# Layer norm of the next batch in two halves on ScalarE, its statistics in front of the output addition, the router's exponential one step later, rounding in front of gelu, and the output stored in quarters

## The chip, the core and the metric

One core of a Trainium2 chip runs the whole program. The time is the device time of one execution in microseconds (us); lower is better. The engines are TensorE (PE in the rows; its weight loads are PEld), VectorE (DVE), ScalarE (ACT), GpSimd (POOL) and SyncE (SP, which here only issues DMAs). Each works through its own list of instructions in order, and waits on semaphores.

## The reference

Everything is float32. There are 4 batches of 512 tokens with 256 features. In the attention part a query sees the 65 keys `i-64 <= j <= i`; the context gives keys and values.

```python
x = x + tanh(g_xattn) * attention(layernorm(x), ctx, wq, wk, wv, wo)   # 16 heads of 64, rotary, window 64
h = layernorm(x)
shared = einsum('tse,she->th', gelu(h @ shared_up), shared_down)       # 2 shared experts, 128 wide
probs  = softmax(h @ router_w.T)                                       # 16 routed experts
gate   = probs where among the 4 largest, else 0
routed = einsum('tre,rhe->th', gelu(h @ routed_up) * gate, routed_down)
x = x + tanh(g_ffn) * (shared + routed)
```

The kernel computes every one of the 18 experts for every token and multiplies a routed one by its gate, which is 0 for most tokens.

## The kernel before

**Products.** Every float32 operand of a projection is split into a rounded part (`xTh`, `wh`, `oTh`, made by ScalarE) and the rest (`xTl`, `wl`, `oTl`, a subtraction on VectorE or GpSimd), and each product is three matmuls (`product`, line 827).

**Attention.** Work is cut into 16 units `u` (batch `b = u // 4`, group of 4 heads `g`), and each unit into 4 steps, so that there are 64 steps `c` (one head each), with `k = c % 4` and a few steps to drain. A list `steps` says which jobs go with each step, and every engine walks through the same list. For head `c`: PE makes the scores (`psS`, L990; two heads at a time, at even `c`), VectorE takes the row maxima (L781), ScalarE the exponentials (L563), VectorE inverts their sum (L791), GpSimd divides (L422), PE transposes (`psT`, L1002), ScalarE copies them (`pT`, L572), PE multiplies by the values (`psO`, L1021), ScalarE rounds the result (`oTh`, L578) and VectorE makes its rest (`oTl`, L795). Jobs `q`, `k`, `v` are the next unit's projections, job `y` the output projection of the unit before, whose result VectorE adds to `x` (L749). PE writes the jobs into two pairs of banks, `ring`.

**Layer norm of batch `b+1`** is made while batch `b` is in attention: job `stat` (VectorE: L630, L633, from `x`; then four small GpSimd instructions, L446 to L455, which make `rstd` and `shift`), job `norm` (ScalarE, four ACTIVATEs `xn<-x,shift,rstd`, L553), job `xT` (PE transposes `xn`, ScalarE rounds, VectorE makes the rest). The layer norm of the expert part has the same jobs with `n = B + b`; the first of them, `n = B = 4`, falls into the attention of the last batch (steps 53, 55 and 59).

**The last unit** (steps 60 to 63) also holds the router of batch 0: `r` (PE L967; four VectorE instructions up to `lex`, L670, semaphore `r_sub`; then the exponential `lexp` on ScalarE, L544), `pick_a` and `pick_b` (VectorE, the four largest), `gT` (PE transposes the gate).

**Experts.** 72 experts `n` (18 in each batch) follow each other. On PE expert `n` is `up(n)` (6 matmuls 128x512, `ring[0]`) and then `down(n - 2)` (12 matmuls 128x256 into the sums). In between come ScalarE's `gelu(n)` (L495, `act_g`, shown as `sneg`), VectorE's multiplication by the gate (`gated`, L706, `prob<-sneg,arena`, routed experts only), ScalarE's rounding (`round_gated`, L511, `oTh`) and VectorE's rest (`rest_gated`, L714, `oTl`, semaphore `f_lo`, for which `down` waits). `round_gated(n)` also waits for `down(n - 2)`, which read the same buffer. Table `after` puts the jobs of the next batch's layer norm and router behind certain experts. At a batch's end VectorE adds the sums to `x` in two halves (job `z`, L770) and SyncE stores each half.

ScalarE has to load a function table (`ACT_TABLE_LOAD`) when it goes from exponential to gelu and back. The copies and the rounding need none.

## Time and profile before

| | |
|---|---|
| runs, median (lowest to highest) | 548.89 us (548.44 to 549.3), 3 runs |
| the profiled execution: its own time | 548.71 us |
| the profiled execution: span from the first to the last instruction | 546.9 us |
| PE busy | 517.7 us, 95% |
| PEld, DVE, ACT, POOL busy | 84%, 60%, 56%, 52% |
| chain that ended last | PE 77%, POOL 9%, DVE 5%, issue 4%, ACT 3% |
| mean granted TensorE clock | 0.984 |

The profiled execution's own time is 1.8 us above its span, and 0.2 us under the median. A share of the whole span says little here: what matters is in which stretches PE stands still, and for whom. A matmul's end is modelled, and matmuls overlap, so that the wait that a row shows in brackets is a little less than what was lost.

### The profile page before, as it was taken

To read this page: it belongs to the slowest core of one execution; us is meant where nothing else is said; L and a number is where in the kernel's file an instruction comes from. 1 tells how busy PE (TensorE), PEld (TensorE's weight loads), DVE (VectorE), ACT (ScalarE), POOL (GpSimd) and SP (SyncE) were. 2 spreads that over 40 slices of the span, in tenths; PEclk is the share of its full clock that TensorE was granted. 3 is DMA by queue.
4 is the path that set the end of the run, shared out by engine and by line. 5 is a ranking of instruction groups with operands and counts; after the bars stand their busy time and mean duration, and the time that the engine had idled before them with its cause. 6 is when DMAs were issued, how large, how long until landed. Compare 5 with 4: busy or idle time off the path is not lost.

```text
span 546.9 us, 13117 instructions
## 1 busy us (share of the span) xinstructions
PE 517.7 (95%) x4906; PEld 457.7 (84%) x4906; DVE 327.7 (60%) x1047; ACT 306.5 (56%) x860; POOL 284.7 (52%) x231
## 2 busy tenths in 40 slices
PE   7667989999999999999999889999999999999997
PEld 5556878998899888988889778989998999899996
DVE  5866756566756676657565736564555455544444
ACT  3264666566675657766666575764454445444332
POOL 4668999797889778988797635440100010000000
PEclk9997999999999999999999799999999999999999
DMA  7422224110131011102111237305400450054001
GB/s 251 163 74 59 58 62 145 35 37 1 35 112 36 2 37 35 37 15 61 35 37 31 61 101 266 96 27 180 170 1 0 151 199 2 1 178 172 0 1 38
DMA packets 20173, 41.02 MB, mean 75 GB/s; under 512 B 2896, under 2 KB 3152, under 8 KB 20112
## 3 DMA queue, kind: packets, MB, share of 16 engines
q1 hardware_dynamic: 20112, 40.20, 23.4%
q8 instruction: 39, 0.64, 0.5%
q14 instruction: 22, 0.18, 0.1%
HBM read 30.62 MB, written 2.23 MB: 60 GB/s over the span
## 4 chain that ended last, share of the span: by engine, by line
PE 77%; POOL 9%; DVE 5%; issue 4%; ACT 3%; DMA 1%; POOLq 0%; ACTq 0%; DVEq 0%
PE ring L827 52%; PE psS L827 9%; PE psO L1021 6%; PE psS L990 5%; PE psT L1002 4%; POOL arena L416 2%; POOL prob L422 2%; POOL arena L418 2%; POOL arena L406 1%; POOL wl L430 1%; DVE arena L656 1%; PE psT L967 1%; POOL arena L409 1%; DVE oTl L714 1%; ACT pT L572 1%
## 5 line engine op out<-in xcount | busy, mean ns | idle before, releaser
L827 PE MATMUL ring<-xTh,wh 128*128 128x512 f32 x272 | 111.3, 409 | 3.3 <-DVE wl L727 1.7
L827 PE MATMUL ring<-xTh,wl 128*128 128x512 f32 x272 | 107.3, 394 | 0.0
L827 PE MATMUL ring<-xTl,wh 128*128 128x512 f32 x272 | 106.9, 393 | 0.0
L495 ACT ACTIVATE sneg<-ring 128x512 f32<-128x512 f32 x72 | 43.2, 600 | 102.1 <-PE ring L827 99.4
L706 DVE TENSOR_TENSOR prob<-sneg,arena 128x512 f32<-128x512 f32 x64 | 44.8, 699 | 75.1 <-ACT sneg L495 73.4
L827 PE MATMUL ring<-wh,oTh 128*128 128x256 f32 x272 | 78.3, 288 | 1.7 <-DVE oTl L714 0.9
L827 PE MATMUL ring<-wl,oTh 128*128 128x256 f32 x272 | 76.8, 282 | 0.0
L827 PE MATMUL ring<-wh,oTl 128*128 128x256 f32 x272 | 76.6, 282 | 0.0
L422 POOL TENSOR_TENSOR prob<-prob,rinv 128x512 f32<-128x512 f32 x64 | 66.7, 1042 | 14.9 <-DVE rinv L791 14.8
L827 PEld LDWEIGHTS ring<-xTh,wh 128*128 128x128 f32 x272 | 51.3, 189 | 13.3 <-issue 3.2
L827 PEld LDWEIGHTS ring<-xTh,wl 128*128 128x128 f32 x272 | 51.2, 188 | 12.0
L827 PEld LDWEIGHTS ring<-xTl,wh 128*128 128x128 f32 x272 | 51.4, 189 | 7.2
L563 ACT ACTIVATE prob<-sneg,nmax 128x128 f32<-128x128 f32 x128 | 49.6, 391 | 12.6 <-DVE nmax L781 12.6
L827 PEld LDWEIGHTS ring<-wh,oTh 128*128 128x128 f32 x272 | 51.2, 188 | 4.6 <-DVE oTl L714 1.5
L572 ACT ACTIVATE pT<-psT 128x512 f32<-128x512 f32 x64 | 37.9, 592 | 30.0 <-PE psT L1002 30.0
L430 POOL TENSOR_TENSOR wl<-raw,wh 128x512 fp32r<-128x512 f32 x27 | 37.4, 1391 | 32.6 <-ACT wh L524 32.6
L563 ACT ACTIVATE prob<-arena,nmax 128x128 f32<-128x128 f32 x128 | 49.7, 395 | 5.2 <-DVE nmax L781 3.5
L827 PEld LDWEIGHTS ring<-wl,oTh 128*128 128x128 f32 x272 | 51.3, 189 | 1.5
L827 PEld LDWEIGHTS ring<-wh,oTl 128*128 128x128 f32 x272 | 51.3, 189 | 0.0
L714 DVE TENSOR_TENSOR oTl<-prob,oTh 128x512 fp32r<-128x512 f32 x64 | 45.0, 703 | 6.3 <-ACT oTh L511 6.3
L578 ACT ACTIVATE oTh<-psO 128x512 fp32r<-128x512 f32 x32 | 19.2, 600 | 52.0 <-PE psO L1021 52.0
L749 DVE SCALAR_TENSOR_TENSOR x<-ring,tg,x 128x1024 f32<-128x1024 f32 x16 | 20.5, 1284 | 46.1 <-PE ring L827 46.1
(117 smaller groups left out, 1268.6 us busy)
## 6 DMA issues: line engine op xcount, KB each, us to landing
arena<-gate_scratch SPq DMA_DIRECT2D x64, 256.0 KB, 6.6
raw<-in_e SPq DMA_DIRECT2D x18, 256.0 KB, 2.6
raw<-in_w SPq DMA_DIRECT2D x16, 256.0 KB, 3.0
arena<-arena SPq DMA_DIRECT2D x16, 256.0 KB, 3.1
arena<-arena SPq DMA_DIRECT2D x16, 192.0 KB, 3.5
craw<-in_ctx SPq DMA_DIRECT2D x4, 512.0 KB, 4.2
x<-in_x SPq DMA_DIRECT2D x4, 512.0 KB, 4.0
out<-x SPq DMA_DIRECT2D x8, 256.0 KB, 2.7
```

The lines of the kernel that those rows point to most:

```text
L422: pool.tensor_tensor(prob[:, c % BUFS, :, :], prob[:, c % BUFS, :, :], rinv[:, c % BUFS, :].unsqueeze(2).to_broadcast([P, TT, P]), ALU.mul ...
L430: pool.tensor_tensor(wl[:, slot(n), :], raw[:, n % RAW, :], wh[:, slot(n), :].bitcast(F32), ALU.subtract).then_inc(w_lo_p, 1)
L495: act.activation(act_g[:, n % 2, :], ring[0][:, n % 2, :], ACT.Gelu).then_inc(f_gelu, 1)
L563: last = act.activation(prob[:, c % BUFS, t, :], sneg[c % BUFS][:, t, :], ACT.Exp, bias=nmax[:, c % 4, t:t + 1], scale=-1.0, accum_out=rsu ...
L572: act.activation(pT[:, c % 4, :, :], psT[:, :, :], ACT.Copy).then_inc(p_out, 1)
L706: dve.tensor_tensor(act_f[:, n % 2, :], act_g[:, n % 2, :], gate_bc[:, r, :], ALU.mult).then_inc(f_mul, 1)
L714: dve.tensor_tensor(lo, src[:, n % 2, :], hi.bitcast(F32), ALU.subtract).then_inc(f_lo, 1)
L749: dve.scalar_tensor_tensor(x[:, b, :, :].rearrange("p t d -> p (t d)"), both_banks(job)[:, :, :].rearrange("p a n -> p (a n)"), tg[:, 0:1] ...
L827: last = pe.matmul(out, a, b, start=start and i == 0 and j == 0, stop=stop and i == n - 1 and j == 2, skip_group_check=check)
L990: last = pe.matmul(psS[odd][e * W:(e + 1) * W, t, :], qT[rows, u % 2, h // 2, blk * W:(blk + 1) * W], kT[rows, u % 2, h // 2, blk * W:(blk ...
L1002: last = pe.transpose(psT[:, t, :], prob[:, c % BUFS, t, :], ident[:, :])
L1021: last = pe.matmul(psO[h * DH:(h + 1) * DH, blk * W:(blk + 1) * W], v[:, u % 2, t, head * DH:(head + 1) * DH], pT[:, (2 * p + h) % 4, t, e ...
```

## The change

- Attention: job `stat` of the next batch now stands in front of job `y` in step `k = 3, g = 1`; `norm` is cut into `norm_a` (step `k = 0, g = 2`) and `norm_b` (step `k = 1, g = 2`), two ACTIVATEs each. For the first layer norm of the expert part `stat` moves from step 53 to 51 (in front of `y`), `norm` from step 55 to halves at 52 and 53.
- The router's exponential becomes a job of its own, `rexp`: for batch 0 it goes from the end of step 60 to step 61, behind the copy of the transposed probabilities; for the other batches from behind expert 9 to behind expert 10. The layer norm's jobs among the experts each go one expert later.
- `expert(n)`: ScalarE rounds expert `n-1` before it takes gelu of `n`, and VectorE makes the rest of `n-1` before it multiplies `n` by its gate.
- PE issues the `up` of the last expert together with that of the one before.
- `z` and the stores go in four quarters (128x256) instead of two halves.

```diff
+            if (k, g) == (3, 1) and b + 1 < B:
+                jobs.append(("stat", b + 1))
+            if c == CHUNKS - 13:
+                jobs.append(("stat", B))
             if k == 3 and u >= 1:
                 jobs.append(("y", u - 1))
...
-            if k == 3 and g == 1 and b + 1 < B:
-                jobs.append(("stat", b + 1))
             if k == 0 and g == 2 and b + 1 < B:
-                jobs.append(("norm", b + 1))
-            jobs += {(UNITS - 3, 1): [("stat", B)], (UNITS - 3, 3): [("norm", B)],
+                jobs.append(("norm_a", b + 1))
+            if k == 1 and g == 2 and b + 1 < B:
+                jobs.append(("norm_b", b + 1))
+            jobs += {(UNITS - 3, 0): [("norm_a", B)], (UNITS - 3, 1): [("norm_b", B)],
...
-            for e, kind in ((2, "stat"), (4, "norm_a"), (5, "norm_b"), (7, "xT"), (9, "r"), (11, "pick_a"),
-                            (12, "pick_b"), (14, "gT")):
+            for e, kind in ((3, "stat"), (5, "norm_a"), (6, "norm_b"), (8, "xT"), (9, "r"), (10, "rexp"),
+                            (11, "pick_a"), (12, "pick_b"), (14, "gT")):
...
             def expert(n):
+                if 1 <= n <= N:
+                    round_gated(n - 1)
                 if n < N:
                     gelu(n)
-                if 1 <= n <= N:
-                    round_gated(n - 1)
...
+                if c == CHUNKS - 3:
+                    do(("rexp", 0))
...
             def expert(n):
+                if 1 <= n <= N:
+                    rest_gated(n - 1)
                 if n < N and experts[n][1] >= NS:
                     gated(n)
-                if 1 <= n <= N:
-                    rest_gated(n - 1)
...
-                    for half in range(2):
-                        dve.wait_ge(down_pe, 2 * NE * (n + 1) - 1 + half)
+                    for t in range(TT):
+                        dve.wait_ge(down_pe, 2 * NE * (n + 1) - 1 + t // 2)
...
             def expert(n):
-                if n < N:
+                if n < N - 1:
                     up(n)
+                if n == N - 2:
+                    up(n + 1)
                 if n >= 2:
                     down(n - 2)
```

ScalarE around the first layer norm of the expert part, steps 55 and 56 before, 52 and 53 now (`xn` is the layer norm, `pT` the copy for which PE's values wait). Before:

```order
L553 ACTIVATE xn<-x,shift,rstd 128x256 [waits xT_pe,ln_rstd]
L553 ACTIVATE xn<-x,shift,rstd 128x256 x3
L572 ACTIVATE pT<-psT 128x512 [waits oT_pe,p_pe]
L578 ACTIVATE oTh<-psO 128x512 [waits y_pe,oT_pe]
L563 ACTIVATE prob,rsum<-sneg,nmax 128x128 [waits p_pe,s_max]
```

Now:

```order
L556 ACTIVATE xn<-x,shift,rstd 128x256 [waits xT_pe,ln_rstd]
L556 ACTIVATE xn<-x,shift,rstd 128x256
L575 ACTIVATE pT<-psT 128x512 [waits oT_pe,p_pe]
L566 ACTIVATE prob,rsum<-sneg,nmax 128x128 [waits p_pe,s_max]
L566 ACTIVATE prob,rsum<-sneg,nmax 128x128 x3
L556 ACTIVATE xn<-x,shift,rstd 128x256 [waits xT_pe,ln_rstd]
L556 ACTIVATE xn<-x,shift,rstd 128x256
L575 ACTIVATE pT<-psT 128x512 [waits oT_pe,p_pe]
```

Four ACTIVATEs stood in front of one copy; now two stand in front of each of two copies, one step apart.

ScalarE among the experts of a middle batch, around the router's exponential (`sneg` is gelu's output, `oTh` the rounding). Before:

```order
L495 ACTIVATE sneg<-ring 128x512 [waits f_lo,up_pe]
L511 ACTIVATE oTh<-prob 128x512 [waits down_pe,f_mul]
L544 ACT_TABLE_LOAD
L544 ACTIVATE lexp<-lex 128x64 [waits r_sub]
L495 ACT_TABLE_LOAD [waits f_lo]
L495 ACTIVATE sneg<-ring 128x512 [waits up_pe]
L511 ACTIVATE oTh<-prob 128x512 [waits down_pe,f_mul]
```

Now:

```order
L514 ACTIVATE oTh<-prob 128x512 [waits down_pe,f_mul]
L498 ACTIVATE sneg<-ring 128x512 [waits f_lo,up_pe]
L547 ACT_TABLE_LOAD
L547 ACTIVATE lexp<-lex 128x64 [waits r_sub]
L514 ACTIVATE oTh<-prob 128x512 [waits down_pe,f_mul]
L498 ACT_TABLE_LOAD [waits f_lo]
L498 ACTIVATE sneg<-ring 128x512 [waits up_pe]
L514 ACTIVATE oTh<-prob 128x512 [waits down_pe,f_mul]
```

The rounding of an expert now stands in front of the next expert's gelu, one of them between the two table loads, and the exponential stands one expert later.

PE near the end of the program: the end of `up(70)` (`xTh,wh` and its like, 128x512) and what follows it. Before:

```order
L827 MATMUL ring<-xTh,wh 128x512
L827 MATMUL ring<-xTl,wh 128x512
L827 MATMUL ring<-xTh,wl 128x512
L827 MATMUL ring<-wh,oTh 128x256 [waits f_lo]
L827 MATMUL ring<-wl,oTh 128x256
```

Now:

```order
L832 MATMUL ring<-xTh,wh 128x512
L832 MATMUL ring<-xTl,wh 128x512
L832 MATMUL ring<-xTh,wl 128x512
L832 MATMUL ring<-xTh,wh 128x512 [waits f_gelu]
L832 MATMUL ring<-xTl,wh 128x512
```

`down(68)` stood behind `up(70)`; now `up(71)` stands there, and all four of the last `down`s stand behind it.

## Rows read from the trace of the kernel before

**Rows 1.** Windows: length, busy of PE, PEld, DVE, ACT, POOL; granted clock; DMA share, GB/s
```profile
52.50:92.50 40.00, 36.78 (x440) 32.04 (x439) 26.15 (x101) 28.50 (x93) 39.24 (x32) 1.00 0.30 85
92.50:272.50 180.00, 180.00 (x2185) 159.99 (x2184) 118.11 (x470) 116.72 (x410) 150.61 (x113) 1.00 0.15 39
```

**Rows 2.** Timeline of PE, early attention: start, length, instruction, [idle before, releaser]
```profile
91.53 0.47 PE L827 MATMUL ring<-xTh,wh 128*128 128x512 f32 x1 [0.29 <-POOL xTl L435]
```

**Rows 3.** Timeline of PE, steps 55 and 56: its waits there
```profile
279.55 0.36 PE L827 MATMUL ring<-wh,oTh 128*128 128x256 f32 x1 [0.62 <-DVE oTl L795]
282.79 0.65 PE L1002 MATMUL psT<-ident,prob 128*128 128x128 f32 x4 [0.16 <-POOL prob L422]
285.01 1.15 PE L1021 MATMUL psO<-pT,arena 128*64 128x64 f32 x32 [0.54 <-ACT pT L572]
```

**Rows 4.** Timeline of DVE and of ACT, steps 51 to 55
```profile
264.17 1.28 DVE L749 SCALAR_TENSOR_TENSOR x<-ring,tg,x 128x1024 f32<-128x1024 f32 x1 [3.73 <-PE ring L827]
275.26 1.40 DVE L630 BATCH_NORM_STATS2 stats<-x 128x6 f32<-128x256 f32 x4
...
273.36 0.60 ACT L572 ACTIVATE pT<-psT 128x512 f32<-128x512 f32 x1 [1.09 <-PE psT L1002]
282.41 2.07 ACT L553 ACTIVATE xn<-x,shift,rstd 128x256 f32<-128x256 f32 x4
```

**Rows 5.** Timeline of PE, steps 60 to 63
```profile
309.22 1.09 PE L1002 MATMUL psT<-ident,prob 128*128 128x128 f32 x4 [1.45 <-ACT pT L572]
310.24 1.99 PE L990 MATMUL psS<-arena 64*64 64x128 f32 x32
315.64 0.36 PE L827 MATMUL ring<-wh,oTh 128*128 128x256 f32 x1
```

**Rows 6.** Timeline of ACT, steps 60 and 61
```profile
308.34 0.26 ACT L544 ACTIVATE lexp<-lex 128x64 f32<-128x64 f32 x1 [0.77 <-DVE lex L670]
308.50 0.58 ACT L572 ACTIVATE pT<-psT 128x512 f32<-128x512 f32 x1
...
311.04 0.58 ACT L572 ACTIVATE pT<-psT 128x512 f32<-128x512 f32 x1
```

**Rows 7.** Windows, columns as in rows 1: the stretch of the lower clock
```profile
308.25:314.75 6.50, 5.53 (x72) 4.55 (x73) 4.29 (x36) 3.85 (x14) 2.83 (x3) 0.50 0.15 45
```

**Rows 8.** Chain that ended last: start, length, what
```profile
494.68 43.86 PE ring L827 x276
```

**Rows 9.** Timeline of PE, end of `up(11)` and start of `down(9)` in batch 2
```profile
468.96 0.40 PE L827 MATMUL ring<-xTl,wh 128*128 128x512 f32 x1
469.19 0.40 PE L827 MATMUL ring<-xTh,wl 128*128 128x512 f32 x1
469.90 0.39 PE L827 MATMUL psS<-wh,oTh 128*128 128x256 f32 x1 [0.32 <-DVE oTl L714]
```

**Rows 10.** Timeline of ACT, behind expert 9 of batch 1
```profile
411.79 0.26 ACT L544 ACTIVATE lexp<-lex 128x64 f32<-128x64 f32 x1 [1.72 <-DVE lex L670]
412.06 1.28 ACT L495 ACT_TABLE_LOAD   x1
413.36 0.60 ACT L495 ACTIVATE sneg<-ring 128x512 f32<-128x512 f32 x1
```

**Rows 11.** Timeline of ACT, DVE and PE, the last two experts and the end
```profile
538.56 0.60 ACT L495 ACTIVATE sneg<-ring 128x512 f32<-128x512 f32 x1 [1.73 <-PE ring L827]
540.05 0.63 ACT L511 ACTIVATE oTh<-prob 128x512 fp32r<-128x512 f32 x1 [0.38 <-PE ring L827]
...
539.19 0.69 DVE L706 TENSOR_TENSOR prob<-sneg,arena 128x512 f32<-128x512 f32 x1 [1.55 <-ACT sneg L495]
540.72 0.69 DVE L714 TENSOR_TENSOR oTl<-prob,oTh 128x512 fp32r<-128x512 f32 x1 [0.23 <-ACT oTh L511]
542.98 1.46 DVE L770 SCALAR_TENSOR_TENSOR x<-ring,tg,x 128x512 f32<-128x512 f32 x2 [1.57 <-PE ring L827]
...
540.54 0.39 PE L827 MATMUL ring<-wh,oTh 128*128 128x256 f32 x1 [0.58 <-DVE oTl L714]
```

More of the change, by code:

```diff
@@ L360, in store @@
             def store(b):
-                for half in range(2):
-                    sp.wait_ge(z_out, 2 * b + half + 1)
-                    sp.dma_start(out_d[b][:, 2 * half:2 * half + 2, :],
-                                 x[:, b, 2 * half:2 * half + 2, :]).then_inc(out_done, 16)
+                for t in range(TT):
+                    sp.wait_ge(z_out, TT * b + t + 1)
+                    sp.dma_start(out_d[b][:, t, :], x[:, b, t, :]).then_inc(out_done, 16)
             def do(job):
@@ L382, in _ @@
                 do(job)
-            sp.wait_ge(out_done, 16 * 2 * B)
+            sp.wait_ge(out_done, 16 * TT * B)
         @block.gpsimd
@@ L541, in do @@
                     expert(n)
-                elif kind == "r":
+                elif kind == "rexp":
                     act.wait_ge(r_sub, n + 1)
@@ L766, in do @@
                 elif kind == "z":
-                    for half in range(2):
-                        dve.wait_ge(down_pe, 2 * NE * (n + 1) - 1 + half)
-                        tokens = x[:, n, 2 * half:2 * half + 2, :].rearrange("p t d -> p (t d)")
-                        dve.scalar_tensor_tensor(tokens, sums(n, half), tg[:, 1:2], tokens,
+                    for t in range(TT):
+                        dve.wait_ge(down_pe, 2 * NE * (n + 1) - 1 + t // 2)
+                        dve.scalar_tensor_tensor(x[:, n, t, :], sums(n, t // 2)[:, t % 2 * D:t % 2 * D + D],
+                                                 tg[:, 1:2], x[:, n, t, :],
                                                  ALU.mult, ALU.add).then_inc(z_out, 1)
@@ L884, in down @@
                     if b >= 2:
-                        pe.wait_ge(z_out, 2 * (b - 1))
+                        pe.wait_ge(z_out, TT * (b - 1))
                     elif b:
```

## The prediction

> **What bounds the kernel now.** I read the windows first. From 92.5 to 272.5 us PE is busy for all of 180.00 us at full clock [rows 1]: nothing that another engine does there shows in the time unless PE comes to wait. Among the experts the chain of waits has one piece of 276 matmuls in 43.86 us [rows 8]; an expert has 18, so one takes 2.86 us and PE is again the bound. What can be won is the time in which PE waits, so I took PE's timeline and kept the rows with a bracket. In a row of matmuls one starts .23 us after the other although each lasts .40 (468.96, 469.19); the one behind the wait should start at 469.42 and starts at 469.90, so a bracket of .32 has cost .48 [rows 9]. I add this refill (.05 to .16) to each bracket. PE waits in five places: before 91.5 us, at 279 to 285, at 304 to 325, four times among the experts, and before the last two `down`s.
>
> **The early layer norm (steps 7 to 9): 0.** PE has 3.2 us without work from 52.5 to 92.5, some of it behind ScalarE's four `xn`, which are now two and two. But GpSimd is busy for 39.24 of these 40 us [rows 1], and what PE waits for at the end, at 91.53, is GpSimd's `xTl` [rows 2]. The change gives GpSimd the same instructions in nearly the same order. PE comes there earlier and waits longer. If GpSimd were not the wall, the gain would be up to 3; I take 0, since the 0.8 us that GpSimd does not work are scattered, and allow 0.4. Batches 2 and 3 have their layer norms in the stretch without a wait: 0, too.
>
> **The layer norm for the experts (now steps 51 to 53): -1.55.** Three waits: .62 for `oTl` behind the statistics on VectorE, .16 for a division, .54 for `pT` behind the four `xn` (282.41 to 284.48) [rows 3, 4]. With refill (.07, .16, .06) that is 1.6. In the new places: VectorE stands idle 3.73 us before the output addition at 264.17, and the statistics (1.40 and the aggregation, under 2 in all) fit into that; the addition is not late [rows 4]. GpSimd's `rstd` and `shift` come two steps earlier and are out of the way of the division. On ScalarE two `xn` take half of 2.07, 1.04 us. The first two run in the idle time before a `pT`. The second two stand before the `pT` at 273.36, which has 1.09 us of idle time in front of it [rows 4]: all but used up by 1.04, so I leave a new wait of .05, up to .4 if `shift` comes late. 1.6 - .05 = 1.55.
>
> **The router's exponential in the last unit: -0.7 or -1.75.** PE stood idle 1.45 us, from 307.77 to 309.22 [rows 5], because `pT` of head 58 was queued behind the exponential, which waited for `lex` until 308.34 and let `pT` start at 308.50 [rows 6]. Now `pT` goes first and starts at about 307.8: .7 us earlier. The second `pT` (311.04) stands behind a softmax and a weight rounding and moves by some .35 only, to an end at 311.25. What follows hangs on the clock. In this stretch, 308.25 to 314.75, the granted clock is .50, the 1.2 GHz level [rows 7]; it fell after PE had run the router's 16 matmuls of 32 columns and then stood idle. At this clock the transposes and the scores (1.99 us) hide the wait for the second `pT`, and the gain is .7. If the clock stays up, transposes and scores are over at about 310.05, PE waits until 311.25 for `pT`, values take 1.1, then `oTh` and `oTl` .60 and .69 with hand-over, and the output projection, before at 315.64 [rows 5], starts at 313.9: the gain is 1.75. PE still runs the 16 narrow matmuls and still stands .7 us behind them, so I take the fall as the likelier: .7. Later waits there (the first gelu's table load) move along unchanged.
>
> The Trainium skill, TensorE: Matmul & The Clock Gate, Part 1, says that the gate follows how busy TensorE has been, not the program; by this rule either outcome is open, and it would make the sum 1.05 larger if the clock held. The rows at .50 agree with a gate that answers to idleness.
>
> **The experts: -1.8.** Four waits for `f_lo`, at `down(3)` of batch 0 and `down(9)` of batches 0, 1 and 2, of .45 to .48 with refill, 1.9 together; the last of them stands in [rows 9]. An `up` takes six times .23, so a `down` about 1.45. Counted from the end of `up(n)`, `down(n)` starts at 5.7. Before, the rounding stood behind gelu(n+1) and the rest behind the next gate, which ends at 2.86 + 1.5: rest done at 5.05, a cushion of .65. Now: gelu until .8 (.60 long), gate until 1.5 (.69), rounding until 2.25 (.63; it may start when `down(n-2)` is over, at about 1.6), rest until 3.0; gelu of `n+1` starts at 3.05, so the rounding in front does not delay it. The cushion grows to 2.7. What is queued behind the rounding is gelu, behind that `up` two experts later; neither is late while the loop gelu, gate, rounding (.60 + .69 + .63 and hand-overs, 2.1) stays below 2.86. The exponential no longer waits for `lex` (1.72 us before [rows 10]), but its two table loads now stand behind gelu(10) and behind round(10): counted from the end of `up(10)`, load 0.7 to 2.0, exponential to 2.3, rounding to 2.9, load to 4.2, gelu(11) to 4.8, gate to 5.5, `pick_a` (1.2 us) to 6.7, rest(11) to 7.4; `down(11)` starts at 8.5. In batch 0, with weight roundings between and a slower `pick_a`, rest(11) ends at about 8.5: no cushion, for which I take .1, at most .4. The transposes `xT` come one expert nearer to the router; their rests end about .2 before PE needs them, so again 0 to .2 for each batch.
>
> In the trace gelu starts .02 us after the table load of 1.28 [rows 10]. The Trainium skill, ScalarE: Activation LUTs, What ACT_TABLE_LOAD costs, gives 1283 ns for the load, and agrees, but 1380 ns of drain with it, which no row here shows. By the page every switch would hold ScalarE 1.4 us longer; that is the last rival's story.
>
> **The end: -0.05.** Before, `down(70)` waited .58 (.74 with refill) and `down(71)` started 1.45 later, at 541.98 [rows 11]. Now both `up`s are over at 538.36 less one `down` (1.45), at 536.9, and `down(68)` ends at 538.35. Round(70) needs `down(68)`: 538.5 to 539.15; rest(70) to 539.85; `down(70)` starts at 539.9, .65 earlier. But gelu(71), which could start at 537.1, is queued behind round(70): to 539.65; its gate stands behind rest(70): to 540.5; rounding to 541.15, rest to 541.85; `down(71)` starts at 541.9. The wait has moved from one `down` to the other and .05 is won. This is a price of rounding first together with the early `up`.
>
> **Stores in quarters: 0.** Two halves of `z` take 1.46 us [rows 11]. A width of 1024 takes 1.28 [rows 4], of 512 .73, so 256 about .46, and two of them .2 more than one half. The last store then starts .2 later with half the bytes; from the end of `z` (544.44) to the end of the span (546.9) a half's store took 2.4. Bounds: .2 of a loss if bytes cost nothing, .4 of a gain if they cost as in a rate fitted to these. I take 0.
>
> **Sum.** 1.55 + .7 + 1.8 + .05 = 4.1 off the profiled execution's 548.7: 544.6. Against the median, .2 higher, 544.8; I say **544.6**.
>
> **Rivals.**
> - *Forecast: all waits named go, the clock falls again.* 543.9 to 545.3. Chance .50.
> - *The clock holds in the last unit.* For it: .75 us less idling behind the router's matmuls. Against: the narrow matmuls stay, and a new wait of 1.2 us follows. 544.6 - 1.05 = 543.5. Chance .24.
> - *The waits come back in part.* Norm_b late by .4, batch 0 without cushion (.4), `xT` late three times (.6), and PE's longer wait before 91.5 brings the low clock there, which would make some of PE's work after it late by about 1. 544.6 + 2.2 = 546.8. For it: each cushion is .2 or less. Chance .14.
> - *The change does nothing*: the waits at 279 and among the experts turn up elsewhere in full, e.g. because VectorE, not ScalarE's order, sets `f_lo`. 548.7. Chance .04.
> - *Slower: the table switch costs more in its new place*, between two roundings. If each load held ScalarE 1.28 longer, gelu(11) and rest(11) would be 2.56 later: waits of 2.5, 1.5 and 1.5 in the three batches, 544.6 + 5.5 = 550.1. It makes the kernel slower than before once the extra passes about 1.0 us for a load. Against it: .02 [rows 10]. Chance .08.
>
> **Numbers.** What a measurement of this kernel can tell from no change is about 0.2% (1.1 us). Faster: .50 + .24 + .14 = .88; same .04; slower .08. The range 543.0 to 546.9 holds the first three.
>
> **What the changed profile would show.** No bracket for `oTl` or `pT` on PE at the place of `norm` (now about 270 to 275); a bracket before the transposes behind the router of .7 instead of 1.45, and in the windows the clock level there; no `f_lo` bracket among the experts except perhaps at `down(11)` of batch 0; PE still released by GpSimd's `xTl` near 91.5; a bracket of up to .6 at `down(71)` and about .1 at `down(70)`. The forecast is wrong if PE waits before `r`, if GpSimd's stretch gets shorter, or if brackets appear behind the table loads.

## The result, and the profile after

| | before | after |
|---|---|---|
| runs of one chip, median (lowest to highest) | 548.95 us (548.44 to 549.33), 7 runs | 545.16 us (544.74 to 547.05), 7 runs |
| ratio, 95% interval | | 0.9942 [0.9925, 0.9958] |
| profiled execution: own time, span | 548.71, 546.9 | 545.07, 543.2 |
| PE, DVE, ACT, POOL busy | 95%, 60%, 56%, 52% | 95%, 62%, 58%, 52% |
| mean granted clock | 0.984 | 0.991 |

The changed kernel is faster by 0.58%. The runs of after lie on two levels, four at 544.7 to 545.2 (clock .991 or .987) and three at 546.7 to 547.1 (.981); the profiled one is of the lower.

The windows of after, columns as in [rows 1]; the last one is the stretch behind the router, which answers to [rows 7]:

```profile
52.50:92.50 40.00, 36.87 (x440) 32.03 (x439) 26.84 (x102) 29.26 (x96) 38.78 (x31) 1.00 0.30 84
92.50:272.50 180.00, 180.00 (x2185) 160.00 (x2184) 119.46 (x477) 117.05 (x408) 152.28 (x118) 1.00 0.15 39
307.25:313.25 6.00, 3.79 (x76) 3.02 (x77) 5.69 (x36) 4.75 (x21) 2.84 (x3) 1.00 0.14 46
```

PE's timeline of after, six of its waits from 92 us on (start, length, instruction, [idle before, releaser]):

```profile
92.04 0.47 PE L832 MATMUL ring<-xTh,wh 128*128 128x512 f32 x1 [1.10 <-POOL xTl L438]
...
307.25 0.63 PE L1009 MATMUL psT<-ident,prob 128*128 128x128 f32 x4 [0.78 <-ACT pT L575]
...
309.88 1.15 PE L1028 MATMUL psO<-pT,arena 128*64 128x64 f32 x32 [0.97 <-ACT pT L575]
...
313.27 0.36 PE L832 MATMUL ring<-wh,oTh 128*128 128x256 f32 x1 [1.27 <-DVE oTl L800]
...
366.45 0.39 PE L832 MATMUL psS<-wh,oTh 128*128 128x256 f32 x1 [0.23 <-DVE oTl L719]
...
538.09 0.38 PE L832 MATMUL ring<-wh,oTh 128*128 128x256 f32 x1 [0.30 <-DVE oTl L719]
```

The three waits of [rows 3] are gone, and so are the four for `f_lo` at their old places [rows 9]. New are .97 and 1.27 us in the last unit, behind one of .78 that was 1.45 [rows 5], and .23 in batch 0 of the experts, in front of `down(12)`. The wait before the last two `down`s has moved from one to the other [rows 11].

To see where the 3.64 us between the two profiled executions lie, I cut each profile at four of its rows: (1) PE's wait for `xTl` near 92 us; (2) the start of the values in step 60 (before 304.23, after 302.93, bracket .65 in both); (3) the output projection of the last unit (315.64, 313.27); (4) the first `z` of the last batch (542.98, 539.10). The table has the time at (1), then the distances, then from (4) to the execution's own time. The experiments stand in it too. "Low clock" is from when to when the granted clock stood at .50 in the last unit (the 1.2 GHz level); I call those of e1, e4, e5 and e11 short, the others long.

| profiled execution | at (1) | (1) to (2) | last unit (2) to (3) | low clock there | experts (3) to (4) | end | own time |
|---|---|---|---|---|---|---|---|
| before | 91.53 | 212.70 | 11.41 | 308.1 to 314.9 | 227.34 | 5.73 | 548.71 |
| after | 92.04 | 210.89 | 10.34 | none | 225.83 | 5.97 | 545.07 |
| e1 | 92.24 | 212.71 | 10.63 | 309.5 to 312.9 | 224.54 | 5.72 | 545.84 |
| e2 | 93.24 | 210.88 | 11.39 | 306.9 to 313.8 | 227.33 | 5.73 | 548.57 |
| e3 | 92.59 | 212.69 | 11.20 | 308.2 to 315.0 | 229.28 | 5.72 | 551.48 |
| e4 | 92.26 | 210.88 | 10.35 | 307.7 to 311.1 | 225.72 | 5.98 | 545.19 |
| e5 | 91.89 | 210.92 | 10.89 | 308.6 to 312.0 | 225.25 | 5.97 | 544.92 |
| e6 | 92.37 | 210.90 | 11.29 | 305.9 to 312.7 | 226.17 | 5.96 | 546.69 |
| e7 | 91.84 | 210.83 | 10.35 | none | 225.72 | 5.90 | 544.64 |
| e8 | 91.77 | 210.92 | 10.35 | none | 225.25 | 5.91 | 544.20 |
| e9 | 92.28 | 210.88 | 11.29 | 305.8 to 312.6 | 225.24 | 5.72 | 545.41 |
| e10 | 93.52 | 210.84 | 11.17 | 307.3 to 314.1 | 225.13 | 5.71 | 546.37 |
| e11 | 92.35 | 210.91 | 10.35 | 307.8 to 311.2 | 225.17 | 5.92 | 544.70 |
| e12 | 94.33 | 210.92 | 11.20 | 308.2 to 315.0 | 224.58 | 5.70 | 546.73 |

Between before and after: +.51 up to (1), of which .28 is there before the first changed job, at the first `wl` on GpSimd (50.42, 50.70); -1.81, -1.07, -1.51, and +.24 at the end. Column (1) to (2) takes two values, .02 and .09 wide, and tells a part's worth far more sharply than a time of the whole kernel. After, e4 and e8 to e12 have the same program up to (3): what differs between them up to there, 2.56 us at (1) and .95 in the last unit, is no effect of an edit. The column of the experts is less sharp than (1) to (2): after, e4 and e7 have the same program from (3) on and show 225.83, 225.72 and 225.72, so a part of .1 us can't be told there.

Part of the scatter at (1) shows in the granted clock before it. In every profile it stands at .50 for 7 to 10 us, beginning between 38 and 42 us, and in half of them also for a shorter stretch before 32 us. Only e2, e10 and e12 have the early stretch together with one of 10 us (e12: 28.3 to 31.7 and 41.9 to 52.1), and they came to (1) last, at 93.24, 93.52 and 94.33; all others were there by 92.59.

### The profile page after: what moved, and what is told of

Same layout as the page of the kernel before. It is cut to its first block, busy times and chain, and to the rows that moved or that the text cites. A ratio compares the mean times of both kernels' runs of the same rounds, so it can differ in the third digit from the quotient of the medians.

```text
span 543.2 us, 13137 instructions
## 1 busy us (share of the span) xinstructions
PE 515.0 (95%) x4906; PEld 456.2 (84%) x4906; DVE 335.1 (62%) x1055; ACT 312.7 (58%) x860; POOL 284.9 (52%) x231
## 4 chain that ended last, share of the span: by engine, by line
PE 79%; POOL 10%; DVE 4%; issue 3%; ACT 2%; DMA 1%; SPq 0%; DVEq 0%; POOLq 0%; ACTq 0%
PE ring L832 54%; PE psS L832 9%; PE psO L1028 6%; PE psS L997 5%; PE psT L1009 4%; POOL arena L419 2%; POOL arena L421 2%; POOL prob L425 2%; POOL wl L433 1%; POOL arena L409 1%; POOL arena L412 1%; DMA x<-in_x 1%; PE psT L974 1%; DVE arena L661 1%; DVE prob L711 1%
## 5 line engine op out<-in xcount | busy, mean ns | idle before, releaser
L514 ACT ACTIVATE oTh<-prob 128x512 fp32r<-128x512 f32 x64 | 40.4, 631 | 49.8 <-PE ring L832 21.2
L711 DVE TENSOR_TENSOR prob<-sneg,arena 128x512 f32<-128x512 f32 x64 | 47.2, 738 | 29.0 <-ACT sneg L498 28.8
```

Of the source, the lines that this page charges most:

```text
L514: act.activation(gated_parts(n)[0], src[:, n % 2, :], ACT.Copy).then_inc(f_hi, 1)
L711: dve.tensor_tensor(act_f[:, n % 2, :], act_g[:, n % 2, :], gate_bc[:, r, :], ALU.mult).then_inc(f_mul, 1)
```

## The experiments

e1 to e8 ran on one chip, e9 to e11 on a second and e12 on a third. Each ratio is against runs of before on the same chip: e1 to e4 share theirs (median 549.50), as do e5 to e8 (549.23) and e9 to e11 (549.55); e12 has 549.34. Medians of different chips are not to be compared to a few tenths.

**e1: rounding first, alone.** The kernel before, with `round_gated(n - 1)` in front of `gelu(n)` and `rest_gated(n - 1)` in front of `gated(n)`, nothing else.

```diff
             def expert(n):
+                if 1 <= n <= N:
+                    round_gated(n - 1)
                 if n < N:
                     gelu(n)
-                if 1 <= n <= N:
-                    round_gated(n - 1)
```

> The kernel before with one part of the change: ScalarE rounds expert n-1 in front of gelu of n, and VectorE makes its rest in front of the gate. Theory A (the rounding's place feeds PE): all four waits for f_lo among the experts go (1.9 us), down(71) starts about .6 earlier because up(71) is not issued early, and the last unit stays as it was, low clock included: 548.9 - 2.5 = 546.4. Rival B (the waits came from the exponential's place, which is left here): the three waits at down(9) stay and only the one of .45 at down(3) goes: 548.4.

546.20 us (545.84 to 547.5, 5 runs), ratio 0.9949 [0.9937, 0.9961]. All four `f_lo` waits and the one at the end are gone; the experts take 2.80 less than before. That is theory A for the waits; but the last unit did not stay as it was, its stretch of low clock was a short one and it took .78 less, while (1) came .71 later, so that the 546.4 expected was met partly by chance. The 2.80 are also 1.29 more than in the changed kernel (1.18 against e4): something there gives part of it back.

**e2: the layer norm in the attention, alone.** Only the jobs `stat`, `norm_a`, `norm_b` of the steps are moved.

```diff
-                jobs.append(("norm", b + 1))
-            jobs += {(UNITS - 3, 1): [("stat", B)], (UNITS - 3, 3): [("norm", B)],
+                jobs.append(("norm_a", b + 1))
...
+            jobs += {(UNITS - 3, 0): [("norm_a", B)], (UNITS - 3, 1): [("norm_b", B)],
```

> The kernel before with the layer norm moves of the attention alone: stat in front of y, norm in halves, the expert part's first one at steps 51 to 53. Theory A: the waits of 1.6 us at 279 to 285 go, none of the 3 us that PE lacks before 91.5 is given back because GpSimd is the wall, and the last unit keeps its low clock: 547.2. Rival B (the early part counts as well): 544.5 to 546. Rival C (the clock in the last unit is set by how this part shifts it): in some runs 2 us less.

547.68 us (546.57 to 548.68, 10 runs), ratio 0.9967 [0.9956, 0.9978]. (1) to (2) is 210.88, the value of after: the 1.82 us come from this part alone. The stretch of low clock in the last unit was a long one, as before, and the unit took what it took before. By place this is theory A. But the ten runs lie in two groups, five at 546.6 to 547.1 (mean clock .983 to .987) and five at 548.3 to 548.7 (.980 or .981), with the profile in the second: the 2 us less in some runs that rival C expected were seen too, and the median lies between the groups. No profile of the faster group was taken, so that where it wins them is not shown.

**e3: the exponential later, alone.** `rexp` behind expert 10 and in step 61; the rest as before.

```diff
-(9, "r"), (11, "pick_a"),
+(9, "r"), (10, "rexp"), (11, "pick_a"),
...
+                if c == CHUNKS - 3:
+                    do(("rexp", 0))
```

> The kernel before with the exponential moved alone: step 61 behind the copy for batch 0, behind expert 10 for the others; rounding stays behind gelu. Theory A: the wait behind the router in the last unit falls by .7, and by 1.1 to 3 where the clock holds there; among the experts the wait only moves, from down(9) to down(10), since two table loads stand in front of gelu(11) and round(10) stands behind it: the three waits of .48 become .5 to 1.0. Together 547.0 to 548.9. Rival B (the exponential's place removes the experts' waits by itself): 546.9 with a low clock, 545 without, and no wait for f_lo among the experts.

550.65 us (549.96 to 551.68, 6 runs), ratio 1.0026 [1.0015, 1.0037]: slower. Neither theory allowed more than 548.9. In the last unit it wins .21, among the experts it loses 1.94, in its profile mostly by two of PE's waits in batch 0 (theory A had the waits move to the new place, but at .5 to 1.0 each, and one for a batch):

```profile
365.01 0.39 PE L829 MATMUL psS<-wh,oTh 128*128 128x256 f32 x1 [0.93 <-DVE oTl L716]
...
369.09 0.39 PE L829 MATMUL psS<-wh,oTh 128*128 128x256 f32 x1 [1.02 <-DVE oTl L716]
```

**e4: the changed kernel again**, on the chip of e1 to e8.

> The changed kernel once more, to see its two levels of time. Theory A: they are the clock in the last unit. Runs at about 545.0 have a mean granted clock of .991, runs at about 547.0 have .981, with nothing in between but .5 us of noise, and a profile of a slow one shows the level of .50 behind the router's matmuls, at least 10 us of it. Rival B: the levels come from elsewhere (the beginning, a DMA); then the profile's difference lies before 300 us.

545.53 us (544.79 to 547.15, 6 runs), ratio 0.9934 [0.9922, 0.9947]. The six times go in the order of their mean clock: 544.79 at .991, 545.02 and 545.19 at .987, 545.87 and 545.95 at .984, 547.15 at .981. So the time goes with the clock, but not on two levels with nothing between, as theory A had it; and of the 547.15 there is no profile. In its last unit the clock fell at 307.7 and was back at 311.1, and the unit still took 10.35, as in after, where it held:

```profile
307.75:311.00 3.25, 3.25 (x50) 2.59 (x50) 3.01 (x18) 2.29 (x10) 1.94 (x2) 0.50 0.00 0
```

**e5: the changed kernel with the exponential at its old places.**

```diff
-(8, "xT"), (9, "r"), (10, "rexp"),
+(8, "xT"), (9, "r"),
...
-                elif kind == "rexp":
+                elif kind == "r":
```

> The changed kernel with the router's exponential alone put back to its two old places: at the end of step 60, and behind expert 9. The exponential moved alone made the kernel before slower by about 1.4 us, so it is open what it is worth beside the other parts. Theory A (the parts help each other: with rounding first, the exponential one expert later costs ScalarE nothing, and in the last unit it frees pT): without the move PE waits about 1.45 us again for pT behind the router's matmuls instead of .78, and the stretch of low clock starts there; 0 to .3 lost among the experts; 545.5 + .7 to + 2 = 546.2 to 547.5. Theory B (the later exponential is a loss among the experts in any company, because lex would have to wait less than its table load): 545.5 - 1.4 + .7 = 544.8 or less, with no wait at down(11) of batch 0.

544.96 us (544.48 to 546.78, 6 runs), ratio 0.9930 [0.9905, 0.9956]. Neither theory: the wait behind the router is 1.45 again and the unit .54 longer, the experts are .58 shorter (.47 against e4), without the bracket at `down(12)`. Where both places are moved, the two cancel. The multiplication that is stretched beside GpSimd (e11 below) is there all the same; it only starts .60 earlier, counted from (3), and the rest of expert 12 .58 earlier:

```profile
362.84 1.79 DVE L709 TENSOR_TENSOR prob<-sneg,arena 128x512 f32<-128x512 f32 x1
...
365.56 0.68 DVE L717 TENSOR_TENSOR oTl<-prob,oTh 128x512 fp32r<-128x512 f32 x1
```

**e6: `pick_b` one step later** (step 62, `gT` in 63), to free VectorE in front of the row maxima.

```diff
-(UNITS - 1, 1): [("pick_a", 0), ("pick_b", 0)], (UNITS - 1, 2): [("gT", 0)]
+(UNITS - 1, 1): [("pick_a", 0)], (UNITS - 1, 2): [("pick_b", 0)], (UNITS - 1, 3): [("gT", 0)]
```

> The changed kernel with pick_b one step later (step 62) and gT behind it (step 63). Theory A: the new wait of 1.27 us (.77 in a second profile) in front of the output projection of the last unit comes from VectorE, where pick_b's work of 1.15 us stands in front of the row maxima and of oTl; then oTl ends about 1.15 earlier, the bracket falls to .1 or less, and the time falls by .7 to 1.2, less what gT in a later step costs the first experts (up to .5 where the first routed expert waits for its gate): 544.3 to 544.9 on a chip where the changed kernel takes 545.5. Rival B: ScalarE's second copy pT and its rounding are what is late, VectorE is only last in line: the bracket stays above .8 and the time is the same within .3. Rival C: the gate now comes late for the first routed expert and the gain turns into a wait of 1 us or more there: 545.5 to 546.5.

546.19 us (544.43 to 547.6, 8 runs), ratio 0.9939 [0.9918, 0.9960]. The profiled execution had the clock at .50 from 305.9 to 312.7, and in such a stretch the maxima start late for another reason, the scores (1.99 long):

```profile
309.30 1.99 PE L997 MATMUL psS<-arena 64*64 64x128 f32 x32
...
311.43 0.29 DVE L786 CUSTOM_DVE_ANT_0 arena<-psS,mask 128x128 f32<-128x128 f32 x1 [1.99 <-issue]
...
313.72 0.69 DVE L800 TENSOR_TENSOR oTl<-psO,oTh 128x512 fp32r<-128x512 f32 x1 [0.42 <-ACT oTh L581]
```

The unit took 11.29, like e9 with the same stretch and without the edit; the experts took .34 more than after. The edit loses there; what it is worth at a held clock, for which it was meant, this profile doesn't show. One run of it has a mean clock of .991 and took 544.43, where e4's took 544.79: too little to go by.

**e7: three dummy matmuls of 128 columns** behind the router's.

```diff
-(UNITS - 1, 1): [("pick_a", 0), ("pick_b", 0)],
+(UNITS - 1, 1): [("warm", 3), ("pick_a", 0), ("pick_b", 0)],
```

> The changed kernel with three more matmuls of 128 columns on a constant tile, which nothing reads, issued by PE in step 61 into its idle time behind the router's matmuls and in front of the transposes that wait for pT. Theory A (the time of a run goes with how PE idles behind the narrow matmuls: the clock falls there in some executions and holds in others): with the gap filled the clock falls less often; the median moves to the lower of the two levels seen (about 545.0 instead of 545.5), the runs scatter less (no run at 547), and the stretch of low clock at 308 to 311 is gone from the profile. Rival B (the narrow matmuls themselves, or work before them, bring the fall, or it doesn't hang on what stands there): two levels remain, 545.0 and 547.0, in about the same shares, plus 0 to .3 us for the added matmuls.

544.83 us (544.64 to 546.49, 6 runs), ratio 0.9924 [0.9902, 0.9946]. They filled the gap: PE ran them from 306.05 to 306.88, and the bracket in front of the transposes is gone. The clock held in the profile, but two runs of six lie at 546.0 and 546.5. With three of seven and one of six at 546.7 or more without the dummies, that decides nothing.

**e8: `up(71)` back behind `down(68)`.**

```diff
-                if n < N - 1:
+                if n < N:
                     up(n)
-                if n == N - 2:
-                    up(n + 1)
```

> The changed kernel with up(71) back behind down(68). Theory A (the early up costs what rounding first gains at the end, because round(70) waits for down(68), which stands behind up(71), and gelu(71) is queued behind it): down(68) ends 1.45 us earlier, gelu(71) becomes the later of the two; down(71) starts .5 to .6 us earlier after down(68) than in the changed kernel: 545.5 - .55 = 544.95, and no bracket or one below .1 at down(70). It agrees with the kernel before with rounding first alone, which showed no wait at the end. Rival B (the chain gelu, gate, rounding, rest of expert 71 is what the end waits for, wherever up(71) stands, and it then starts 1.45 us later): the same or up to .6 us slower, 545.5 to 546.1, with a bracket at down(71).

544.66 us (544.03 to 546.4, 6 runs), ratio 0.9920 [0.9896, 0.9943]. PE has no bracket left at the end, and the experts take .58 less than after (.47 less than e4): theory A. First ScalarE and VectorE of after, then the same operations of e8:

```profile
534.68 0.63 ACT L514 ACTIVATE oTh<-prob 128x512 fp32r<-128x512 f32 x1 [2.27 <-PE ring L832]
535.22 0.58 ACT L498 ACTIVATE sneg<-ring 128x512 f32<-128x512 f32 x1
...
536.67 0.63 ACT L514 ACTIVATE oTh<-prob 128x512 fp32r<-128x512 f32 x1 [0.87 <-DVE prob L711]
537.34 0.69 DVE L719 TENSOR_TENSOR oTl<-prob,oTh 128x512 fp32r<-128x512 f32 x1 [0.70 <-ACT oTh L514]
```

```profile
533.03 0.63 ACT L514 ACTIVATE oTh<-prob 128x512 fp32r<-128x512 f32 x1 [0.91 <-PE ring L832]
...
534.37 0.60 ACT L498 ACTIVATE sneg<-ring 128x512 f32<-128x512 f32 x1 [0.71 <-PE ring L832]
...
535.87 0.63 ACT L514 ACTIVATE oTh<-prob 128x512 fp32r<-128x512 f32 x1 [0.90 <-PE ring L832]
```

In after, rounding of expert 70 waits 2.27 us for `down(68)`, which stands behind the early `up`, and gelu of 71 starts behind it. In e8 gelu of 71 waits for its own `up` and the chain to the last rest ends .81 earlier (.23 of it from the start of the execution).

**e9: e8 with `z` and stores in halves.**

```diff
-                for t in range(TT):
-                    sp.wait_ge(z_out, TT * b + t + 1)
+                for half in range(2):
+                    sp.wait_ge(z_out, 2 * b + half + 1)
```

> The changed kernel with up(71) back behind down(68), and z and the stores in halves again. The early up alone undone gave 544.66 beside 545.5 of the changed kernel on this chip. Theory A (a quarter costs .10 more than half a half, 1.66 us for two against 1.46, and a smaller last store wins nothing: 128 KB landed in 2.8 us, 256 KB in 2.7): .2 less than with quarters, 544.4 to 544.5, and from the first z to the end of the span .2 less. Rival B (the last store's bytes do count; the rate between the two sizes is hidden by other stores in the median): from the end of z to the end of the span it takes .2 to .4 longer than in quarters, the sum 544.6 to 544.9.

544.78 us (544.42 to 545.41, 4 runs), ratio 0.9912 [0.9898, 0.9927]. The end takes 5.72, as before, against 5.91 in e8: two quarters of `z` more cost .2, and the smaller last store gives nothing. From the end of `z` to the end of the span it is 2.4 us here, in e8 and in after. Theory A, by place.

**e10: e9 with the layer norm's jobs among the experts at their old places.**

```diff
-(3, "stat"), (5, "norm_a"), (6, "norm_b"), (8, "xT"),
+(2, "stat"), (4, "norm_a"), (5, "norm_b"), (7, "xT"),
```

> The kernel of the run above, with the layer norm's jobs among the experts back at their old places (stat, norm_a, norm_b, xT behind experts 2, 4, 5, 7 instead of 3, 5, 6, 8). Theory A (xT one expert nearer to the router makes the router's first matmuls of each batch .10 later: 4.61 us instead of 4.52 for that stretch): .3 less in three batches, and in batch 0 the wait at down(12) may shift with the collisions on VectorE: 544.1 to 544.2. Rival B (the later norm is what keeps one of the f_lo waits away; statistics and two xn per expert stood where the waits were): one or more waits of .3 to .5 come back at down(3) of the batches, 544.5 to 545.5.

545.38 us (543.76 to 546.37, 6 runs), ratio 0.9917 [0.9900, 0.9934]. The experts take .11 less (225.13) and no wait came back, so rival B is out. Of theory A's .3 a third is seen, and that is no more than after and e4 differ by with one program; the median is above the 544.1 to 544.2 that it expected.

**e11: GpSimd nearly free in batch 0.**

```diff
-                    pool.tensor_tensor(wl[:, slot(n), :], raw[:, n % RAW, :],
+                    width = 16 if n in late_pieces else L
+                    pool.tensor_tensor(wl[:, slot(n), 0:width], raw[:, n % RAW, 0:width],
```

> The changed kernel, in which GpSimd subtracts only 16 of 512 columns for each piece of weights that it splits during the experts of batch 0; the other 496 columns of wl keep what stood there, so that this part of the computation is left out. Theory A (the one wait left among the experts, .39 at 366.45 us, comes from an operation of VectorE of .69 us that takes 1.78 beside GpSimd's subtraction, ending .55 behind it, twice: at 351.73 and at 363.01): all of L711 and L719 take .68 to .70, and L686 .2 to .3 instead of .87, the wait is gone, and the time falls by .4 to .6: 544.9 to 545.1 against 545.5. Rival B (ScalarE's queue in batch 0, table loads, rounding of weights and gelu, is what makes rest(12) late; the stretched operations fall into its shadow): VectorE's operations get short, but the bracket stays within .1 and the time too.

544.45 us (543.99 to 546.34, 6 runs), ratio 0.9912 [0.9895, 0.9929]. The wait at `down(12)` is gone and the experts take .66 less (.55 less than e4). VectorE, ScalarE and GpSimd of after, in front of `down(12)`, then the same place of e11:

```profile
362.42 1.82 POOL L433 TENSOR_TENSOR wl<-raw,wh 128x512 fp32r<-128x512 f32 x1 [0.58 <-ACT wh L527]
363.01 1.78 DVE L711 TENSOR_TENSOR prob<-sneg,arena 128x512 f32<-128x512 f32 x1
364.82 0.63 ACT L514 ACTIVATE oTh<-prob 128x512 fp32r<-128x512 f32 x1 [2.48 <-DVE prob L711]
...
365.71 0.68 DVE L719 TENSOR_TENSOR oTl<-prob,oTh 128x512 fp32r<-128x512 f32 x1
```

```profile
362.66 0.68 DVE L713 TENSOR_TENSOR prob<-sneg,arena 128x512 f32<-128x512 f32 x1
362.72 0.70 POOL L435 TENSOR_TENSOR wl<-raw,wh 128x16 fp32r<-128x16 f32 x1 [1.66 <-ACT wh L529]
...
364.26 0.68 DVE L721 TENSOR_TENSOR oTl<-prob,oTh 128x512 fp32r<-128x512 f32 x1
```

The gate's multiplication takes .68 instead of 1.78, and rest(12) starts at 364.26 instead of 365.71, 1.79 earlier counted from (3). Theory A.

**e12: the parts that pay.** The changed kernel with e8, halves, the layer norm's jobs and the exponential at their old places among the experts; the exponential of batch 0 stays in step 61. Beside the edits of e8 and e9:

```diff
-(3, "stat"), (5, "norm_a"), (6, "norm_b"), (8, "xT"), (9, "r"), (10, "rexp"),
+(2, "stat"), (4, "norm_a"), (5, "norm_b"), (7, "xT"), (9, "r"), (9, "rexp"),
```

> The changed kernel with the parts taken back that cost something by the runs before: among the experts the layer norm's jobs and the exponential at their old places (stat, norm_a, norm_b, xT behind experts 2, 4, 5, 7, the exponential behind 9), up(71) behind down(68), z and stores in halves. The layer norm in the attention, the exponential in step 61 and rounding before gelu stay. Theory A (the parts add up by place): from xTl near 92 us to the values' wait of step 60 210.9 us; from there to the last unit's output projection 10.35 where the clock holds and 11.2 to 11.3 where it falls by 307; from there to the last z 224.5 to 224.6, as with rounding first alone, with no wait at down(12); from the last z to the end of the run 5.7. From xTl at 91.8 to 92.3 that makes 543.3 to 543.8, and 1.0 to 2 more in executions with more of the low clock: median 543.5 to 544.7 beside 545.5 of the changed kernel. Rival B (what stood at old places collides again with GpSimd's subtractions in batch 0, since the last unit ends at another moment than in the run with rounding first): the experts take 225.1 to 225.8 and the median is 544.3 to 545.5.

545.16 us (543.43 to 546.73, 6 runs), ratio 0.9921 [0.9903, 0.9940]. By place theory A holds: 210.92, 11.20 with a long stretch of low clock, 224.58, 5.70. The profiled execution came to (1) 2.3 us later than after, by a program that is the same up to there, on another chip. 543.43 is the fastest run of all kernels, within the 543.3 to 543.8 expected at a held clock. But the median is above the 543.5 to 544.7 expected and inside rival B's 544.3 to 545.5, though by place the experts did not take rival B's 225.1 or more; and the interval overlaps that of the changed kernel, 0.9934 [0.9922, 0.9947]: that it is better is shown for its places (1.25 + .27 us), not for its time.

## Why the prediction was near, step by step

The forecast of 544.6 (range 543.0 to 546.9) met a median of 545.16. By place:

- **Early layer norm, 0: right.** PE still waits for GpSimd's `xTl` at 92.04, 1.10 us instead of .29 [rows 2]: it came earlier and waited longer, and GpSimd worked 38.78 us of the 40 [rows 1]. That is .46 less than before, which the prediction had named as a sign of error, but it brought no gain. That (1) came .51 later is inside what the same program scatters.
- **Layer norm for the experts, -1.55: right, -1.81 measured** (e2 alone: -1.82). No new wait came of norm_b; two `xn` took 1.09, as reckoned from [rows 4], and `pT` was in time. The rest, .26 more than forecast, is not traced to a row; the three waits seem to cost more than bracket and refill.
- **Last unit, -.7 or -1.75: right up to `pT`, wrong behind it.** The transposes behind the router started .67 earlier, counted from (2) [rows 5], as said, and `pT` came on the predicted chain. What failed is the step "then `oTh` and `oTl` .60 and .69 with hand-over". With the clock held the projection should have started at 313.9, less the 1.30 won up to (2), at 312.6; it started at 313.27, because VectorE was not free for `oTl`. GpSimd, VectorE and ScalarE of after:

```profile
309.43 1.27 POOL L433 TENSOR_TENSOR wl<-raw,wh 128x512 fp32r<-128x512 f32 x1 [1.22 <-ACT wh L527]
309.62 1.15 DVE L700 SCALAR_TENSOR_TENSOR gate<-rep,pr 128x64 f32<-128x64 f32 x1
...
310.70 0.28 DVE L786 CUSTOM_DVE_ANT_0 arena<-psS,mask 128x128 f32<-128x128 f32 x1
...
311.08 0.60 ACT L581 ACTIVATE oTh<-psO 128x512 fp32r<-128x512 f32 x1 [1.25 <-PE psO L1028]
...
312.48 0.65 DVE L800 TENSOR_TENSOR oTl<-psO,oTh 128x512 fp32r<-128x512 f32 x1
```

  The last of `pick_b`'s operations, 128x64 in 1.15 us, ends .07 behind GpSimd's subtraction; then come eight row maxima and only then `oTl`, although `oTh` was there at 311.68. Where GpSimd's subtraction does not meet it, the same operation takes .23 (315.19 in e6, 309.51 in e5): .92 of the 1.15 come from that meeting. I had followed PE and ScalarE and left out VectorE's queue. That moving `pick_b` away, or the subtraction, repairs it is argued, not shown (e6; e11 left this subtraction as it was). The two outcomes that I set apart by the clock do not exist in that form: the unit takes 10.35 where the clock holds and also with a short stretch (e4, e11), where `pick_b` meets GpSimd in the same way and VectorE's queue hides the slower PE, and 11.2 to 11.3 with a long one (e3, e6, e9, e10, e12), where VectorE stands idle in front of the maxima until the scores are there. In the second case the moved exponential is worth .2, not .7 (before against e3). In the first it is .54 by e5, or .28 by e1, which has the old place too and took 10.63; the stretch of e5 fell 5.8 us behind (2), onto the scores and values, that of e1 4.6 us behind it, as in e4 and e11, so that part of the .54 can be the clock's.
- **Experts, -1.8: -1.51 measured, from terms that were wrong in both directions.** Rounding first gives 2.80 with the end (e1), more than the 1.9 of four waits plus the .74 at the last `down`s. Three parts took back 1.27 of the 1.29 that are missing, and with all of them undone e12 comes to 224.58, beside 224.54 in e1. The exponential took .58 (e5; .47 against e4), where I chose .1 and allowed .4: the step "rest(11) ends at about 8.5: no cushion" saw the right batch, but the wait came one expert later, at `down(12)`, and needed two causes. The exponential and its table loads at the new place bring VectorE's queue .6 us later, and VectorE's 1.78 us beside GpSimd makes rest(12) later still. Either one undone removes the wait: in e5 the stretched multiplication stays, in e11 the table loads do. The prediction had only the first. The nearer `xT` took .11 at most (e10), inside 0 to .2 for a batch. The early `up` took .58 (e8; .47 against e4).
- **End, -.05: right.** `down(71)` starts 3.89 earlier than before, as much as the experts ahead of it: the wait moved to it as described and won nothing, "a price of rounding first together with the early `up`". The remaining bracket is .30, half of what I allowed. But the sum looked only at what the swap adds to before: against rounding first without the early `up` it cost .58 (e8).
- **Quarters, 0: +.2 measured, the bound on the side of a loss.** Four `z` took 1.66 against 1.46 for two, .10 more for each half, and the bytes of the last store counted for nothing (2.4 us from the end of `z` to the end of the span, before and after):

```profile
539.10 1.66 DVE L774 SCALAR_TENSOR_TENSOR x<-ring,tg,x 128x256 f32<-128x256 f32 x4 [1.07 <-PE ring L832]
539.61 1.80 SPq L367 DMA_DIRECT2D out<-x  x4
```

The table load was no danger: in after gelu starts .02 us behind its load of 1.28, as in [rows 10], so the last rival's price per load was not paid.

```profile
358.05 1.28 ACT L498 ACT_TABLE_LOAD   x1
359.35 0.60 ACT L498 ACTIVATE sneg<-ring 128x512 f32<-128x512 f32 x1
```

So the total was near partly by luck: 1.81 + 1.07 + 1.51 - .24 - .51 = 3.64, against 4.1, with terms that missed on both sides. The profiled execution showed a held clock, which I had called the less likely, and the gain of neither branch. Of the ten profiles that have the new place of the layer norm and rounding first, the clock held in three (after, e7, e8) and fell in seven, so that the choice itself was not a bad one. The chance of .24 for 543.5 stood for an outcome that VectorE's queue did not allow.

What stays open: what places the stretches of low clock before (1), and with them, it seems, a part of its way from 91.77 to 94.33 with the same program (on three chips), and what decides whether the stretch in the last unit is absent, short or long. No run at 547 of the changed kernel itself was profiled. Its mean clock is .981 there; e10 and e12, the same up to (3), have .981 and .980, with an early stretch, one of 10 us and a long one in the last unit. They suggest that the 2 us are about .9 in the last unit and 1 to 2 before (1).

## What to carry to other kernels

Cut the profiles at a few rows that every version has, and compare the distances: a part of .2 us is seen there, while whole runs scatter by 2. Read the same program twice at the same rows first: its scatter (.09 and .11 here) is the least that such a distance can tell. When a change moves several jobs of the same queues, run each alone and each taken back: the exponential alone made the kernel slower, the early `up` cost about .5, the quarters .2, and the sum still looked like the plan. A wait can need two causes; that undoing one removes it does not clear the other. When a wait is shortened, walk through the queue of every engine behind it, with what stands in front of the needed operation, not only the engine that was named.

## What the runs showed of the hardware

An operation of VectorE with two inputs in SBUF that starts while GpSimd is in an operation does not end before GpSimd does. The traces of after, e5 and e12 have 52 such pairs of single operations up to 400 us; in none did VectorE end first, and the operations of 128x512 ended .50 to .56 behind GpSimd. The multiplication of .68 to .70 us ended .55 behind it (363.01 + 1.78 = 364.79, GpSimd 364.24; in the other pair, 351.73 + 1.76 = 353.49 and 352.94), and with GpSimd down to 16 columns it took .68. It also goes the other way: beginning at 366.54, in the middle of a multiplication that started at 366.32, GpSimd's 1.28 became 1.62; and at 362.42, where a rest of .69 had begun on VectorE at 362.40, it became 1.82:

```profile
351.50 1.44 POOL L433 TENSOR_TENSOR wl<-raw,wh 128x512 fp32r<-128x512 f32 x1 [2.54 <-ACT wh L527]
351.73 1.76 DVE L711 TENSOR_TENSOR prob<-sneg,arena 128x512 f32<-128x512 f32 x1
...
366.32 0.68 DVE L711 TENSOR_TENSOR prob<-sneg,arena 128x512 f32<-128x512 f32 x1
...
366.54 1.62 POOL L433 TENSOR_TENSOR wl<-raw,wh 128x512 fp32r<-128x512 f32 x1 [2.30 <-ACT wh L527]
```

The Trainium skill, SBUF — State Buffer, SBUF: two separate sides, has this rule: VectorE with two SBUF inputs and a GpSimd instruction that reads SBUF contend for one pair of ports, the first to start has it for its whole instruction, and the other blocks. The rows agree but for .12 to .14 us: if the second waited for the whole of the first, the 1.62 would end at 367.00 + 1.28 = 368.28 (it ended at 368.16), the 1.82 at 364.37 (364.24) and the 1.78 at 364.93 (364.79). With the rule in mind the 1.15 of `gate` and the 1.78 in batch 0 could have been looked for in the prediction.

The low clock set in while PE ran the router's narrow matmuls (e6: they end at 306.55, the clock fell at 305.9) or while it stood idle, ran the transposes or the scores behind them (e1 idle, e4 and e11 transposes, e5 scores), and with one and the same program up to (3) it was absent (after, e8), short and without a cost (e4, e11), or long and .9 us dear (e9, e10, e12). What it costs hung on what else was late: in e4 VectorE began the maxima straight behind `gate`, as in after, and in e12 it stood idle .77 us for the scores.
